# Three hops over a sorted graph beside a dense product: dense units dealt anew over the stages, and hop three's carries and selections a tile ahead

## The chip, the cores and the metric

One core of a Trainium2 chip runs the whole program. The metric is the device time of one execution in microseconds (us). Engines: TensorE (PE; its weight loads are PEld), VectorE (DVE), ScalarE (ACT), GpSimd (POOL), and SyncE (SP), which only issues DMAs. Each engine runs its own list of instructions in order and waits at semaphores.

## The reference

x has 100,000 rows (nodes) of 256 numbers. 25,000 edges, sorted by destination, have a source, a destination and a weight.

```python
feats, cur = [x], x
for _ in range(3):                       # three hops
    msgs = edge_weight[:, None] * cur[src]
    cur = segment_sum(msgs, dst, 100000)
    feats.append(cur)
y = concatenate(feats, axis=1) @ shared_weight + output_bias   # (1024, 256)
out = layernorm(x + y)                   # over each row, without scale or shift
```

Only a fifth of the nodes has an incoming edge, so the product of x with the first 256 rows of the weight (to which the kernel adds the identity, for x + ...) is the bulk, and the three other products are needed for few rows.

## The kernel before

**Dense units.** A unit is 512 rows of x (four to a partition); there are 195 and a tail of 160 rows. Per unit: SP loads x (512 KB, `load_ahead`, six units ahead); PE turns it in two pairs of four transposes (`turn_pair`, L1149) and multiplies it in four parts a pair (`multiply_part`, L1158; a part is two instructions of the trace); ACT copies what is turned (`copy_xT`, L887); DVE adds the bias (`copy_y`, L1441) and takes the statistics (L1447, L1456); ACT takes the root and normalises four rows (`normalise`, L900); SP stores the result (`store_before`).

**Tiles.** Edges lie in 197 tiles of 127, padded to 200; row 0 of a tile holds the carry, the partial sum handed on by the tile before. A tile's sum (`sum_tile`, L1188) multiplies a selection matrix (DVE's `select`, L1597, made from a key row of `keys_bc`) by gathered rows `rows_in`. ACT copies row 0 into the next tile's rows (`carry_into`, L946) and the sum out of PSUM (`copy_sum`, L954). POOL issues the gathers and scatters, which are indirect DMAs (L657, L661, L774).

**Stages**, one behind the other on every engine, with dense units as filler between tiles:

1. Tables, 3 steps of 3 units: sorting tables are built, mostly by DVE.
2. Stage A, hop one, 25 steps of 8 tiles (slots q = 0 to 7) and 3 units. Per tile also the turn of c1 (L1215), its product (`multiply_u`, L1221), DVE's copy to u_out (`copy_u`, L1605), a gather of table rows (`look_up`), `match_tail` (L1610), and per step `rows_found` and `stage_gathers`, which wait for eight semaphores. PE's turn of c1 for tile e-1 waits until DVE has copied u of tile e-3.
3. List, 9 steps of 3 units: the edges that later hops need are listed.
4. Stage B, hop two, 5 steps of 8 tiles and 3 units, and one group of 4 tiles without units.
5. Stage C, hop three: 11 groups of 4 tiles (`group_c`) **without units**. Per tile the sum, the turn of a stored c2 row block and of the sum (L1325), ACT's copy of it (L1052), the product (`multiply_v`, L1332), DVE's copy (`copy_v`, L1890), and POOL's adding scatter to u_rows (`scatter_v`).
6. Stage D, 24 steps of 8 tiles, 23 of them with 3 units; in the 24th the tail unit. Rows with an incoming edge are gathered, multiplied, added to u and written over the stored rows: POOL's `scatter_d` waits for the dense stores below it (`await_stores`). A last loop takes late tiles; it runs once here.

c2_rows is filled with zeros by 50 stores of 512 KB (`zero_c2`, L402), which SP issues in the table steps (24) and the list steps (26). They must be there before stage B scatters. The order of work is the order in which the code writes it for each engine: a slot of PE in stage A is

```python
dense_slot(s, par, turn, q)        # three parts, and turns when a pair begins
sum_tile(e, q % 2, q % G, q)
turn_c1(e - 1, (q - 1) % 2, (q - 1) % Q)
multiply_u(e - 2, q % 2)
```

Of the kernel before, what the change touches and what calls it, by code (L numbers as in the profile page):

```python
def gnn_program(nc, x, src, dst, edge_weight, weight, bias, out):
# [25 lines left out]
    STEPS = UNITS // STEP  # L27
    PAIRS = 2 * UNITS + 1
    assert STEPS * STEP == UNITS and STEPS % 2 == 1
# [17 lines left out]
    A0 = 3  # L47
    A_STEPS = TILES // Q
    A_END = A0 + A_STEPS
    LIST0 = A_END + 3  # L50
    LIST_STEPS = 5
    B0 = LIST0 + LIST_STEPS + 1
    B_STEPS = LIST_STEPS
    D0 = B0 + B_STEPS
    D_STEPS = REAL // Q
    FIRST_GROUPS = 2 * LIST_STEPS
# [3 lines left out]
    assert STEPS - D0 == D_STEPS - 1 and A0 % 2 == 1 and D0 % 2 == 0  # L60
    ZERO_FILLS = TILES // G

# [10 lines left out]
    with ctx:  # L73
# [75 lines left out]
        table_idx = [sb(f"table_idx{k}", [P, Q], i32) for k in range(2)]  # L149
# [8 lines left out]
        record = [sb(f"record{k}", [P, Q, FIELDS], bf16) for k in range(2)]  # L158
# [32 lines left out]
        gather_idx = [sb(f"gather_idx{k}", [P, Q], i32) for k in range(2)]  # L191
# [5 lines left out]

        own_c2 = [u_out[:, k, :] for k in range(G)]
# [23 lines left out]

        blank = sem("blank")
# [9 lines left out]
        keys_loaded = sem("keys_loaded")  # L233
# [6 lines left out]
        tail_keys_stored = sem("tail_keys_stored")  # L240
# [44 lines left out]
        list_stored = sem("list_stored")  # L285
# [76 lines left out]

        def unit_rows(ap, u):
            return ap[bass.ds(u * UROWS, UROWS), :].rearrange("(p r) d -> p (r d)", r=RPP)
# [8 lines left out]
        def _(sp):  # L373
# [15 lines left out]
            def store_before(s, par, k):  # L389

                if not isinstance(s, int) or s >= 1:
                    store_unit(STEP * s - STEP + k, STEP * (1 - par) + k)

            def load_ahead(s, par, k):
                u = STEP * s + k + RING
                if not isinstance(u, int) or u < UNITS:
                    load_unit(u, STEP * par + k)
                elif u == UNITS:
                    load_tail()

            def zero_c2(k):
                sp.dma_start(c2_dram[k * UROWS:(k + 1) * UROWS, :].rearrange("(p r) d -> p (r d)", r=RPP),  # L402
                             zeros[:, :]).then_inc(c2_zeroed, 16)

            def load_keys(a, k):

                until(sp, sel_ready, Q * (a - 1))
                sp.dma_start(keys_bc[k][:, :], keys_out_dram[bass.ds(a * (Q * P), Q * P)].partition_broadcast(P)).then_inc(keys_loaded, 16)
# [38 lines left out]
            load_ahead(0, 0, 0)  # L447
            sp.wait_ge(tail_keys_ready, 1)
            sp.dma_start(tail_keys_dram.rearrange("(h p) c -> p h c", h=2), tail_keys[:, :, :]).then_inc(tail_keys_stored, 16)
            sp.wait_ge(keys_stored, 16)  # L450
            load_keys(0, 0)
            sp.wait_ge(blank, 6)
            for k in range(6):
                zero_c2(k)
            for k in (1, 2):
                load_ahead(0, 0, k)
            zeroed = 6
            for s in (1, 2):
                for k in range(STEP):
                    store_before(s, s % 2, k)  # L460
                    load_ahead(s, s % 2, k)
                    for j in range(3):
                        zero_c2(zeroed + j)
                    zeroed += 3


            def step_a(a, s, par, last=False):
                store_before(s, par, 0)
# [12 lines left out]
                load_ahead(s, par, 2)  # L481

            step_a(0, A0, 1)
            with sp.Fori(A0 // 2 + 1, (A_END - 2) // 2) as h:
                for par in range(2):
                    step_a(2 * h + par - A0, 2 * h + par, par)
            step_a(A_STEPS - 2, A_END - 2, 0)
            step_a(A_STEPS - 1, A_END - 1, 1, last=True)


            def dense_step(s):
                for k in range(STEP):
                    store_before(s, s % 2, k)
                    load_ahead(s, s % 2, k)

            s = A_END
            store_before(s, s % 2, 0)
            store_c1(A_STEPS - 1, 1)
            load_ahead(s, s % 2, 0)
            store_u(A_STEPS - 1, 1)  # L500
            for k in (1, 2):
                store_before(s, s % 2, k)
                load_ahead(s, s % 2, k)
            for s in range(A_END + 1, B0):
                if s == LIST0 - 1:
                    sp.wait_ge(listed_copied, A_STEPS)
                    sp.dma_start(list_dram.rearrange("(p t) f -> p (t f)", p=P),
                                 listed[:, :, :].rearrange("p t f -> p (t f)")).then_inc(list_stored, 16)
                for k in range(STEP):
                    store_before(s, s % 2, k)  # L510
                    load_ahead(s, s % 2, k)
                    for j in range(2):
                        if zeroed < ZERO_FILLS:
                            zero_c2(zeroed)
                            zeroed += 1
            assert zeroed == ZERO_FILLS

# [14 lines left out]
            for b in range(B_STEPS):  # L532
                s, t = B0 + b, Q * b
                store_before(s, s % 2, 0)
# [6 lines left out]
                load_ahead(s, s % 2, 0)  # L541
                store_before(s, s % 2, 1)
                load_ahead(s, s % 2, 1)
                store_c2(t, 0, TILES + t + G)
                store_before(s, s % 2, 2)
                load_ahead(s, s % 2, 2)
# [7 lines left out]

            C_TILE = TILES + G * n_groups
            for half in range(2):
# [4 lines left out]
            def group_c(g):  # L561
                for k in range(G):
# [3 lines left out]
                    if k == G - 2:  # L566
                        load_keys2(G * g + G, G, 0, C_TILE + G * g + G)

            load_keys2(0, G, 0, C_TILE)
            group_c(0)  # L570
            with sp.Fori(1, n_groups) as g:
                group_c(g)
# [10 lines left out]
            def step_d(d, s, par):  # L583
                store_before(s, par, 0)
                load_ahead(s, par, 0)
                store_before(s, par, 1)
                if not isinstance(d, int) or d > 0:
                    load_u(2 * d + 3, (2 * par + 3) % 4)
                load_ahead(s, par, 1)
                store_before(s, par, 2)  # L590
                load_ahead(s, par, 2)
                load_u(2 * d + 4, 2 * par)
# [3 lines left out]
            for d in range(2):  # L596
                step_d(d, D0 + d, d)
            with sp.Fori(D0 // 2 + 1, STEPS // 2 - 1) as h:
                for par in range(2):
                    step_d(2 * h + par - D0, 2 * h + par, par)  # L600
            for d in range(D_STEPS - 4, D_STEPS - 1):
                step_d(d, D0 + d, d % 2)
            for k in range(STEP):
                store_before(STEPS, 1, k)
# [4 lines left out]
            load_u(2 * D_STEPS + 1, (2 * D_STEPS + 1) % 4, 1)  # L609
# [1442 lines left out]
```

## Time and profile before

| | |
|---|---|
| median of 3 runs | 1757.12 us (1756.4 to 1757.37) |
| the profiled execution | 1757.15 us, span 1755.4 us |
| PE busy | 1578.4 us, 90% of the span |
| DVE, ACT, POOL busy | 67%, 65%, 61% |
| DMA | 450.85 MB, mean 257 GB/s |
| chain that ended last | PE 77%, DVE 7%, issue 6%, DMA 4% |

Busy time is what an engine spent in instructions that the profile counts. The time stands beside the span: 1.75 us of it lie outside. A row of a timeline has the start in us, the duration, engine, line, operation, output and inputs, a count of merged instructions, and in brackets the idle time before it and what ended that. The chain's shares are of the whole span; what a change is worth is read stage by stage.

### The profile page before, as it was taken

The numbers are of one execution on the slowest core, as the hardware profiler recorded it, in microseconds if no ns is written. First come the engines' busy times: TensorE is split into PE (matmuls) and PEld (weight loads), VectorE is DVE, ScalarE is ACT, GpSimd is POOL, SyncE is SP. The second block draws the span as 40 slices with busy tenths as digits, with TensorE's granted clock in tenths as the row PEclk, the third lists the DMA queues.
The fourth block names the chain that finished last, engine by engine and source line by source line (L and its number), as shares of the span: only waits on it lengthen the run. The fifth ranks groups of instructions, "written<-read, shape, count | busy, mean of one in ns | idle before, by whom it ended". The sixth has DMA issues, their size and how long they took to land.

```text
span 1755.4 us, 37470 instructions
## 1 busy us (share of the span) xinstructions
PE 1578.4 (90%) x8468; PEld 1337.8 (76%) x8468; DVE 1180.8 (67%) x4883; ACT 1147.7 (65%) x3038; POOL 1065.6 (61%) x1043
## 2 busy tenths in 40 slices
PE   6899999999999999998788477777999999999993
PEld 5688888888888888886677265556888888888872
DVE  6767777777777777788766312224777777777773
ACT  3677778777778777665467323324777777777773
POOL 2266656666656666114567756655777777777765
PEclk9899999999999999999899799998999999999997
DMA  8988888888888888798589655546888887888752
GB/s 291 402 300 274 285 284 269 283 277 270 286 285 269 282 279 272 234 389 340 170 297 344 205 112 108 113 98 216 276 275 272 278 275 273 276 277 275 266 198 96
DMA packets 214099, 450.85 MB, mean 257 GB/s; under 512 B 30044, under 2 KB 125593, under 8 KB 214022
## 3 DMA queue, kind: packets, MB, share of 16 engines
q1 hardware_dynamic: 164130, 343.20, 55.9%
q0 software_dynamic: 49456, 106.58, 21.3%
q8 instruction: 29, 0.48, 0.1%
q14 instruction: 48, 0.39, 0.1%
q10 hardware_dynamic: 436, 0.20, 0.0%
HBM read 232.78 MB, written 225.74 MB: 261 GB/s over the span
## 4 chain that ended last, share of the span: by engine, by line
PE 77%; DVE 7%; issue 6%; DMA 4%; POOL 2%; ACT 2%; DVEq 1%; SPq 1%; ACTq 0%; POOLq 0%
PE ps_y L1158 32%; PE ps_u L1221 9%; PE ps_xT L1149 8%; PE ps_sum L1188 7%; PE ps_sum L1366 5%; PE ps_u L1366 5%; PE ps_y L1332 4%; PE ps_u L1215 3%; DVE y_ring L1441 1%; PE ps_u L1360 1%; DVE stats L1447 1%; DMA entries<-listed_edges,list_idx 1%; PE ps_sum L1360 1%; PE ps_xT L1325 1%; DMA c_rows<-sums,scatter_idx 1%
## 5 line engine op out<-in xcount | busy, mean ns | idle before, releaser
L1158 PE MATMUL ps_y<-w_sb,xT 128*128 128x256 f32 x3128 | 810.9, 386 | 19.7 <-DVE y_ring L1441 18.3
L1158 PEld LDWEIGHTS ps_y<-w_sb,xT 128*128 128x128 f32 x3128 | 564.6, 193 | 80.5 <-issue 17.3
L900 ACT ACTIVATE o_ring<-y_ring,shift,rstd 128x256 f32<-128x256 f32 (+1 forms) x782 | 421.8, 590 | 7.3 <-DMA u_rows<-u_out,scatter_idx 7.3
L887 ACT COPY xT<-ps_xT 128x512 f32<-128x512 f32 x391 | 226.5, 579 | 259.5 <-PE ps_xT L1149 259.2
L1441 DVE TENSOR_TENSOR y_ring<-ps_y,bias 128x512 f32<-128x512 f32 x391 | 269.9, 690 | 166.4 <-PE ps_y L1158 159.4
L657 POOL DMA_INDIRECT tails_found<-tail_keys,table_idx x200 | 200.2, 1001 | 234.1 <-PE ps_sum L1188 119.6
L1447 DVE BATCH_NORM_STATS2 stats<-y_ring 128x6 f32<-128x256 f32 (+1 forms) x782 | 290.8, 414 | 3.4
L1149 PE MATMUL ps_xT<-ident,x_ring 128*128 128x128 f32 x1564 | 238.9, 276 | 24.4 <-ACT xT L887 15.5
L1188 PE MATMUL ps_sum<-rows_in,sel 128*128 128x256 f32 x576 | 181.9, 398 | 83.6 <-ACT rows_in L946 43.8
L657 POOL DMA_INDIRECT rows_in<-in_x,gather_idx x200 | 203.5, 1018 | 83.2 <-issue 78.5
L657 POOL DMA_INDIRECT rows_in<-in_x,tailx_idx x197 | 200.0, 1015 | 76.7 <-issue 44.1
L661 POOL DMA_INDIRECT out_rows<-u_out,tailo_idx x197 | 198.4, 1007 | 79.3 <-issue 39.5
L1149 PEld LDWEIGHTS ps_xT<-ident,x_ring 128*128 128x128 f32 x1564 | 193.7, 142 | 68.0 <-ACT xT L887 18.9
L1221 PE MATMUL ps_u<-w_sb,cT 128*128 128x256 f32 x800 | 205.9, 380 | 0.0
L1188 PEld LDWEIGHTS ps_sum<-rows_in,sel 128*128 128x128 f32 x576 | 103.7, 192 | 111.9 <-issue 89.2
L1221 PEld LDWEIGHTS ps_u<-w_sb,cT 128*128 128x128 f32 x800 | 136.7, 191 | 10.2
L1605 DVE TENSOR_TENSOR u_out<-ps_u,bias 128x256 f32<-128x256 f32 x200 | 84.3, 422 | 82.3 <-PE ps_u L1221 81.0
L954 ACT COPY sums<-ps_sum 128x256 f32<-128x256 f32 x288 | 103.5, 359 | 54.2 <-PE ps_sum L1188 45.0
L946 ACT COPY rows_in<-ps_sum 1x256 f32<-1x256 f32 x285 | 100.3, 352 | 51.2 <-PE ps_sum L1188 44.0
L657 POOL DMA_INDIRECT rows_in<-c_rows,gather_idx x92 | 95.0, 1033 | 40.0 <-issue 26.2
L1077 ACT ACTIVATE u_out<-sums,cshift,crstd 128x256 f32<-128x256 f32 x197 | 116.1, 592 | 0.0
L1597 DVE TENSOR_SCALAR sel<-keys_bc,key_in,w 128x128 f32<-128x128 f32 x288 | 101.4, 356 | 16.2 <-issue 7.5
(227 smaller groups left out, 2074.0 us busy)
## 6 DMA issues: line engine op xcount, KB each, us to landing
x_ring<-in_x SPq DMA_DIRECT2D x195, 512.0 KB, 5.9
out_rows<-o_ring SPq DMA_DIRECT2D x195, 512.0 KB, 3.3
c_rows<-zeros SPq DMA_DIRECT2D x50, 512.0 KB, 9.3
c_rows<-sums SPq DMA_DIRECT2D x50, 512.0 KB
u_rows<-u_out SPq DMA_DIRECT2D x50, 512.0 KB, 4.0
keys_bc<-keys_out SPq DMA_DIRECT2D x30, 512.0 KB, 6.8
keys_bc<-u_rows SPq DMA_DIRECT2D x25, 512.0 KB, 5.6
tails_found<-u_rows SPq DMA_DIRECT2D x12, 512.0 KB
```

Of the source, the lines that this page charges most:

```text
L657: pool.indirect_dma_start(dest, None, table, bass.IndirectOffsetOnAxis(ap=index, axis=0), bounds_check=bound, oob_is_err=False).then_inc(s ...
L661: pool.indirect_dma_start(table, bass.IndirectOffsetOnAxis(ap=index, axis=0), source, None, bounds_check=bound, oob_is_err=False).then_inc ...
L887: act.copy(view[0], view[1]).then_inc(xT_copied, 1)
L900: last = act.activation(o_ring[slot][0:rows, r * D:(r + 1) * D], y_ring[k][0:rows, r * D:(r + 1) * D], ACT.Identity, bias=shift[k][0:rows, ...
L1077: act.activation(co[q], cy[q], ACT.Identity, bias=cshift[half][:, k:k + 1], scale=crstd[half][:, k:k + 1]).then_inc(cnormed, 1)
L1149: last = pe.transpose(ps_xT[:, q * P:q * P + rows], x_ring[slot][0:rows, at:at + P], ident[0:rows, 0:rows])
L1158: last = pe.matmul(ps_y[bank][0:rows, r * D:(r + 1) * D], xT[bank][:, q * P:q * P + rows], w_sb[:, c, :], start=c == 0, stop=c == KC - 1)
L1188: pe.matmul(ps_sum[bank][:, 0:D], sel[k][:, :], rows_in[row][:, :], start=True, stop=True).then_inc(summed, 1)
L1221: last = pe.matmul(ps_u[bank][:, D:2 * D], cT[bank][:, c * P:(c + 1) * P], w_sb[:, KC + c, :], start=c == 0, stop=c == KC - 1)
L1366: last = pe.matmul(ps_tail[q % G][:, D:2 * D], cT[q % 2][:, c * P:(c + 1) * P], w_sb[:, c, :], start=c == 0, stop=c == KC - 1)
L1441: dve.tensor_tensor(y_ring[k][0:rows, half * 2 * D:(half + 1) * 2 * D], ps_y[half][0:rows, :], bias2[0:rows, :], ALU.add).then_inc(y_copie ...
L1447: last = dve.bn_stats(stats[k][0:rows, r, :], y_ring[k][0:rows, r * D:(r + 1) * D])
```

## The change

- **Units anew.** Stage A has two units a step instead of three; a bridge of two units stands between B and C; ten of C's eleven groups have two units; all 24 steps of D have three, and the tail unit goes into the step behind. 9 + 50 + 27 + 15 + 2 + 20 + 72 = 195. Steps are now described by (first unit, units, turns of the loop, units of the step before); `unit_at` gives slots. Loops of A hold three steps instead of two.
- **Zero fills.** All 50 are issued in stage A, two a step.
- **Keys of A** come in halves of 256 KB into three buffers instead of 512 KB into two; `record`, `table_idx` and `gather_idx` have three buffers.
- **Stage C.** Its turns and products move to other PSUM banks (ps_u, ps_list) and to the buffer of tails_found, so that ps_xT, ps_y and xT stay with the dense units. ACT's carry and DVE's selection of tile n+1 stand in tile n. Its ten filled groups are written out, the last is a loop.
- **End.** POOL's scatters of the last full step stand ahead of the wait for all stores.

The constants, the steps, and SP's part of stage A:

```diff
-    A0 = 3
+    TABLE_STEPS = 3
+    A_UNIT = STEP * TABLE_STEPS
     A_STEPS = TILES // Q
...
+    C_UNIT = BRIDGE_UNIT + PAIR
+    D_UNIT = C_UNIT + PAIR * FIRST_GROUPS
...
+        def unit_at(off, turns):
+            return off + RING * turns, off % RING, turns + off // RING, off % STEP
...
+        def a_step(i, turns=0):
+            return A_UNIT + PAIR * i, PAIR, turns, STEP if isinstance(turns, int) and i == 0 else PAIR
...
+            def load_keys(a, half, place):
+                until(sp, sel_ready, Q * a + G * half - 2 * G + 1)
...
+                store_behind(dense, 0)
                 if not isinstance(a, int) or a > 0:
                     store_c1(a - 1, 1)
-                if not last:
-                    load_keys(a + 1, par)
-                load_ahead(s, par, 0)
+                if more:
+                    load_keys(a + 1, 0, (place + 1) % 3)
                 if not isinstance(a, int) or a > 0:
                     store_u(a - 1, 1)
-                store_before(s, par, 1)
-                load_ahead(s, par, 1)
+                load_ahead(dense, 0)
+                store_behind(dense, 1)
+                if more:
+                    load_keys(a + 1, 1, (place + 1) % 3)
+                zero_c2(2 * a)
                 store_c1(a, 0)
-                store_before(s, par, 2)
+                load_ahead(dense, 1)
+                zero_c2(2 * a + 1)
                 store_u(a, 0)
-                load_ahead(s, par, 2)
```

POOL, the last scatters:

```diff
             gather_d(LATE0 + G, G, D_STEPS, D_STEPS % 2)
+            await_stores(UNITS - RING, 0)
+            for k in range(Q):
+                scatter_d(LATE0 - Q + k, k, D_STEPS - 1, (D_STEPS - 1) % 2)
             for k in range(RING):
                 pool.wait_ge(stored[k], 16 * (UNITS // RING + (k <= UNITS % RING)))
                 limit(N)
-            for k in range(Q):
-                scatter_d(LATE0 - Q + k, k, D_STEPS - 1, (D_STEPS - 1) % 2)
```

ACT, the bridge and stage C:

```diff
+            dense_step(bridge_step)
...
+            carry_c(0, 0, True)
+            for n in range(G * FIRST_GROUPS):
+                g, k = n // G, n % G
+                dense_slot(c_step(g), 2 * k)
+                copy_sum_c(n, k)
+                if n + 1 < G * FIRST_GROUPS:
+                    carry_c((n + 1) // G, (n + 1) % G)
+                dense_slot(c_step(g), 2 * k + 1)
+                copy_t(n, k)
```

PE, a dense slot, and stage C:

```diff
-                for m in range(3 * q, 3 * q + 3):
+                for m in range(units * q, units * q + units):
...
+                    if dense is not None:
+                        dense_slot(dense, 2 * k)
                     sum_tile(C_TILE + n, k % 2, k, k)
                     if not isinstance(n, int) or n > 0:
                         multiply_v(n - 1, (k - 1) % 2)
+                    if dense is not None:
+                        dense_slot(dense, 2 * k + 1)
                     pe.wait_ge(own_loaded[k], 16 * g + 16)
```

DVE, stage C:

```diff
+            select_c(0, 0)
+            for n in range(G * FIRST_GROUPS):
+                g, k = n // G, n % G
+                products_c(g, k)
+                if n + 1 < G * FIRST_GROUPS:
+                    select_c((n + 1) // G, (n + 1) % G)
+                for q in (2 * k, 2 * k + 1):
+                    dense_slot(c_step(g), q)
```

**PE in stage A**, slots 4 and 5 of the first step (ps_sum is the tile sum, ps_u the turn and product of c1, ps_xT and ps_y the dense turn and parts). Before:

```order
L1149 MATMUL ps_xT<-ident,x_ring4 128x128 x4
L1158 MATMUL ps_y0<-w_sb,xT0 128x256 x3
L1188 MATMUL ps_sum0<-rows_in4,sel0 128x256
L1215 MATMUL ps_u1<-ident,sums 128x128 x2
L1221 MATMUL ps_u0<-w_sb,cT0 128x256 x2
L1158 MATMUL ps_y0<-w_sb,xT0 128x256
L1149 MATMUL ps_xT<-ident,x_ring5 128x128 x4
L1158 MATMUL ps_y1<-w_sb,xT1 128x256 x2
L1188 MATMUL ps_sum1<-rows_in5,sel1 128x256
```

After:

```order
L1209 MATMUL ps_xT<-ident,x_ring4 128x128 x4
L1218 MATMUL ps_y1<-w_sb,xT1 128x256 x2
L1251 MATMUL ps_sum0<-rows_in4,sel0 128x256
L1278 MATMUL ps_u1<-ident,sums 128x128 x2
L1284 MATMUL ps_u0<-w_sb,cT0 128x256 x2
L1218 MATMUL ps_y1<-w_sb,xT1 128x256 x2
L1251 MATMUL ps_sum1<-rows_in5,sel1 128x256
```

Each slot has two parts instead of three, and a turn in every second slot instead of three of four.

**SP's queue in stage A**, the first step. Before:

```order
L387 DMA out_rows<-o_ring0 128x1024
L408 DMA keys_bc1<-keys_out 128x1024
L379 DMA x_ring3<-in_x 128x1024
L387 DMA out_rows<-o_ring1 128x1024
L379 DMA x_ring4<-in_x 128x1024
L412 DMA c1_rows<-sums 128x4x256
```

After:

```order
L449 DMA out_rows<-o_ring0 128x1024
L480 DMA keys_bc1<-keys_out 128x512
L441 DMA x_ring3<-in_x 128x1024
L449 DMA out_rows<-o_ring1 128x1024
L480 DMA keys_bc0<-keys_out 128x512
L473 DMA c2_rows<-zeros 128x1024
L484 DMA c1_rows<-sums 128x4x256
L441 DMA x_ring4<-in_x 128x1024
L473 DMA c2_rows<-zeros 128x1024
L488 DMA u_rows<-u_out 128x4x256
```

One zero fill now stands ahead of the store of c1, and one ahead of the store of u.

**PE in stage C**, one tile and the next sum. Before (in the first group):

```order
L1188 MATMUL ps_sum1<-rows_in1,sel1 128x256
L1332 MATMUL ps_y0<-w_sb,xT0 128x256 x4
L1325 MATMUL ps_xT<-ident,u_out 128x128 x2
L1325 MATMUL ps_xT<-ident,sums 128x128 x2
L1185 REGISTER_ALU
L1188 MATMUL ps_sum0<-rows_in2,sel2 128x256
```

After:

```order
L1251 MATMUL ps_sum1<-rows_in1,sel1 128x256
L1384 MATMUL ps_u1<-w_sb,tails_found 128x256 x4
L1218 MATMUL ps_y0<-w_sb,xT0 128x256 x2
L1377 MATMUL ps_u0<-ident,u_out 128x128 x2
L1377 MATMUL ps_u0<-ident,sums 128x128 x2
L1209 MATMUL ps_xT<-ident,x_ring2 128x128 x4
L1218 MATMUL ps_y1<-w_sb,xT1 128x256 x2
```

Two parts stand between product and turn, and two more, with a dense turn in every tile, between turn and next sum.

## Rows read from the trace of the kernel before

**Rows 1.** The page's 40 slices of the span, PE's busy tenths
```profile
PE   6899999999999999998788477777999999999993
```

**Rows 2.** Windows, us: length; busy (count) of PE PEld DVE ACT POOL; PE clock, DMA share, GB/s
```profile
30.00:45.00 15.00, 10.20 (x55) 8.64 (x54) 13.95 (x49) 7.12 (x15) 1.99 (x2) 0.94 1.03 416
...
125.00:699.00 574.00, 568.59 (x3188) 486.84 (x3188) 426.32 (x1877) 441.18 (x1335) 352.30 (x349) 1.00 0.85 279
...
900.00:960.00 60.00, 55.80 (x291) 46.86 (x289) 41.92 (x155) 45.61 (x120) 46.24 (x46) 1.00 1.00 364
...
990.00:1000.00 10.00, 0.00 (x0) 0.00 (x0) 0.62 (x4) 0.00 (x0) 7.49 (x8) 0.50 0.51 163
...
1010.00:1180.00 170.00, 122.60 (x595) 99.63 (x595) 37.00 (x167) 51.34 (x127) 106.62 (x81) 0.99 0.53 110
```

**Rows 3.** Line L1188 in 120 to 720, then PE's timeline at a step's boundary
```profile
L1188 PE MATMUL ps_sum<-rows_in,sel x364: 378/379/463, 122.2 to 717.1; 128*128 128x256 f32 x182
...
302.58 0.59 PE L1188 MATMUL ps_sum<-rows_in,sel 128*128 128x256 f32 x2
...
304.15 0.63 PE L1149 MATMUL ps_xT<-ident,x_ring 128*128 128x128 f32 x4
304.62 1.46 PE L1158 MATMUL ps_y<-w_sb,xT 128*128 128x256 f32 x6
305.92 0.59 PE L1188 MATMUL ps_sum<-rows_in,sel 128*128 128x256 f32 x2
307.04 0.44 PE L1215 MATMUL ps_u<-ident,sums 128*128 128x128 f32 x2 [0.53 <-DVE u_out L1605]
```

**Rows 4.** PE's timeline in stage C: start, duration, instruction, [idle before]
```profile
1018.65 0.67 PE L1188 MATMUL ps_sum<-rows_in,sel 128*128 128x256 f32 x2 [0.97 <-DVE sel L1597]
1019.16 1.89 PE L1332 MATMUL ps_y<-w_sb,xT 128*128 128x256 f32 x8
1020.88 0.38 PE L1325 MATMUL ps_xT<-ident,u_out 128*128 128x128 f32 x2
1021.10 0.38 PE L1325 MATMUL ps_xT<-ident,sums 128*128 128x128 f32 x2
...
1178.41 0.69 PE L1188 MATMUL ps_sum<-rows_in,sel 128*128 128x256 f32 x2 [1.11 <-ACT rows_in L946]
```

**Rows 5.** DVE's timeline at the same boundary of stage A
```profile
302.78 0.69 DVE L1441 TENSOR_TENSOR y_ring<-ps_y,bias 128x512 f32<-128x512 f32 x1 [0.75 <-PE ps_y L1158]
...
305.79 0.23 DVE L1435 TENSOR_SCALAR gather_idx<-src_node 128x8 int32 x1 [0.80 <-DMA rows_in<-in_x,gather_idx]
...
306.57 0.42 DVE L1605 TENSOR_TENSOR u_out<-ps_u,bias 128x256 f32<-128x256 f32 x1
```

**Rows 6.** POOL's timeline in stage A
```profile
310.81 1.00 POOL L657 DMA_INDIRECT tails_found<-tail_keys,table_idx  x1 [0.30 <-PE ps_sum L1188]
312.11 0.99 POOL L657 DMA_INDIRECT rows_in<-in_x,gather_idx  x1 [0.30 <-issue]
```

**Rows 7.** Timelines from B to C: PE's first sum, POOL's first gather
```profile
1005.62 1.22 PE L1188 MATMUL ps_sum<-rows_in,sel 128*128 128x256 f32 x2 [16.47 <-DVE sel L1597]
...
1002.10 1.04 POOL L657 DMA_INDIRECT rows_in<-c_rows,gather_idx  x1 [2.47 <-issue]
```

**Rows 8.** Timelines: PE at D's first turn and tail unit; POOL at the end
```profile
1197.45 0.69 PE L1360 MATMUL ps_u<-ident,rows_in 128*128 128x128 f32 x2 [12.25 <-DMA rows_in<-in_x,tailx_idx]
...
1700.34 0.44 PE L1149 MATMUL ps_xT<-ident,x_ring 80*128 80x80 f32 x4
...
1719.85 0.98 POOL L661 DMA_INDIRECT out_rows<-u_out,tailo_idx  x1 [0.30 <-DMA out_rows<-o_ring]
...
1735.27 1.05 POOL L657 DMA_INDIRECT rows_in<-in_x,latex_idx  x1 [0.31 <-ACT u_out L1077]
...
1744.50 0.97 POOL L661 DMA_INDIRECT out_rows<-u_out,lateo_idx  x1 [0.49 <-issue]
```

**Rows 9.** The page's DMA issues: the stores of u_out
```profile
u_rows<-u_out SPq DMA_DIRECT2D x50, 512.0 KB, 4.0
```

More of the change, by code:

```diff
@@ L452, in _ @@
-            sp.wait_ge(blank, 6)
[L453 to L468, printed above, removed]
+            for half in range(2):
+                load_keys(0, half, 0)
@@ L469, in step_a @@
+            for k in (1, 2):
+                load_ahead(table_step(0), k)
+            for s in range(1, TABLE_STEPS):
+                store_and_load(table_step(s))
+            sp.wait_ge(blank, 6)
+            def step_a(a, dense, place):
+                more = not isinstance(a, int) or a < A_STEPS - 1
+                store_behind(dense, 0)
                 if not isinstance(a, int) or a > 0:
                     store_c1(a - 1, 1)
-                if not last:
-                    load_keys(a + 1, par)
@@ L813, in scatter_d, with await_stores, step_d @@
                 scatter(out[:, :], co[q], tailo_idx[par][:, q:q + 1], scattered[q // 2])
-            def await_stores(turn, par):
+            def await_stores(off, turns):
                 for k in range(STEP):
-                    pool.wait_ge(stored[STEP * par + k], 16 * turn)
+                    u, slot, turn, place = unit_at(off + k, turns)
+                    pool.wait_ge(stored[slot], 16 * turn + 16)
                     limit(N)
-            def step_d(d, turn, par, gathers=LATE0):
+            def step_d(d, dense, par, turn, gathers=LATE0):
+                off, units, turns, before = dense
                 for q in range(Q):
@@ L977, in _, with step_a @@
             for q in range(4, Q):
-                dense_slot(2, 0, 1, q)
-            def step_a(a, s, par, turn, last=False):
+                dense_slot(table_step(2), q)
+            def step_a(a, dense, place):
                 for q in range(Q):
@@ L1078, in c_normalise, with step_d @@
                                scale=crstd[half][:, k:k + 1]).then_inc(cnormed, 1)
-            def step_d(d, dense=None):
+            def step_d(d, slot=None):
                 for q in range(Q):
@@ L1085, in step_d @@
                         copy_ta(n - 1, (q - 1) % Q)
-                    if dense is not None:
-                        dense(q)
+                    if slot is not None:
+                        slot(q)
                     if q % G == 2 and (not isinstance(g, int) or 0 < g <= -(-REAL // G)):
@@ L1341, in group_c @@
                         multiply_v(n - 1, (k - 1) % 2)
+                    if dense is not None:
+                        dense_slot(dense, 2 * k + 1)
                     pe.wait_ge(own_loaded[k], 16 * g + 16)
@@ L1344, in group_c @@
                     until(pe, t_copied, n)
[L1345 to L1348 removed]
+                    turn_rows(ps_t, (own_c2[k], sums[:, k, :]), t_psum)
+            for g in range(FIRST_GROUPS):
+                group_c(g, c_step(g))
+            with pe.Fori(FIRST_GROUPS, n_groups) as g:
                 group_c(g)
```

624 lines of the change are left out of this document (306 added, 318 removed).

## The prediction

> **What bounds the kernel now.** I read the page's slices first [rows 1]. The digit of PE is 9 nearly everywhere; it drops at the very start, in four or five slices in the middle, and at the end. So TensorE is the bound in most of the kernel, and time can be won only where it stands still. The table by stages says where [rows 2]. In stage A (hop one, 125 to 699) PE is busy 568.6 of 574 us at a granted clock of 1.00. In stage C (hop three, 1010 to 1180) it is busy 122.6 of 170, while DVE (37) and ACT (51) are mostly idle: nothing is full there, it is a chain of waits. At the end of stage B, 990 to 1000, PE does nothing.
>
> Two periods are needed. 182 tiles of stage A begin from 122.2 to 717.1 [rows 3], so a tile takes 594.9/181 = 3.29 us and a step of eight 26.29. In stage C tile sums start at 1018.65 and, 40 tiles on, at 1178.41 [rows 4]: 3.99 us a tile. Between those starts PE's own work is the sum (0.51 to the next start), the product (1.72) and two times two turns (0.22 each), 2.67 us; it waits 1.32 us of each tile, and the row at 1178.41 names ACT's carry, the copy of row 0 for the next sum.
>
> A dense unit costs PE four groups of four turns and sixteen parts. Four turns take 2 x 0.22 = 0.44 [rows 4]; six parts' instructions take 1.30 from 304.62 to 305.92 [rows 3], so a part (two instructions) is 0.433. Two pairs of (0.44 + 4 x 0.433): 4.33 us a unit.
>
> **Part one: stage A, three units to two a step, 25 steps.** PE sheds 4.33 us a step. Not all of it comes back, since PE already waits once a step. Its turn at 307.04 came 0.53 to 0.69 us late, for DVE's copy of u [rows 3]. DVE gets there late because at the end of slot 7 it runs through a copy of y begun at 302.78, statistics, the small copies of rows_found, a pass over eight semaphores ahead of gather_idx at 305.79 (0.80 of idle), and then the copy of u at 306.57 [rows 5]. None of these depends on how many units a step has: slot 7 ends with a pair in both versions. PE needs 3.77 us from the sum at 302.58 to the end of the sum at 305.92 + 0.43, and of this the change takes one part, 0.43 (three parts to two). So the wait grows by 0.43 and the step ends at 26.29 - 4.33 + 0.43 = 22.39. **A: -25 x 3.90 = -97.5 us.** Bounds: nothing lost, -108.3; everything lost (another resource holds the step at 26.29), 0. I take the value near the first end, since PE is the bound in 99% of this stretch.
>
> Can the others keep up at 22.39? POOL issues 16 indirect transfers a step, 1.30 us from start to start [rows 6]: 20.8, so yes, by 1.6 us. ACT's share was 441 of 574 us and it loses a unit's copies too; DVE's was 426 [rows 2]. The DMA volume doesn't fall. A step now moves eleven 512 KB transfers (three loads, three stores, keys, two of c1, two of u), eight gathers of 128 KB and eight of 64 KB: 7.34 MB, and 7.34/26.29 = 279 GB/s, the figure of the row. The change takes out two transfers and puts in two zero fills of the same size, which sat before in the table and list stages. So the step must run at 7.34/22.39 = 328 GB/s. Two rows are near: 900 to 960 ran at 364 GB/s, with POOL's gathers and scatters still issued every 1.3 us, and 30 to 45 at 416 [rows 2]. I price this at nothing; its cover is that x is loaded six units ahead and the stores of c1 and u have four to five slots to land.
>
> The zero fills leave the table and list stages. I take 0 there: the table stage ends with DVE's chain (13.95 of 15 us busy in 30 to 45 [rows 2]), and the list stage is alike. A gain up to 3 us is possible.
>
> **Part two: stage C gets two units a group of four tiles, in ten of eleven groups.** PE's work per tile becomes 2.67 + 2.17 = 4.84 us, more than the 3.99 of today. The 1.32 us wait should vanish: in the new order ACT does carry n+1 directly after copying sum n, DVE selects for n+1 in tile n, and 3 us of other PE work stands between. ACT's work would be 1.2 us a tile as now (51.3 of 170 for 42.6 tiles) and half a unit, at most 3.4 (in A three units and eight tiles together take it 441/574 x 26.29 = 20.2): 4.6, below 4.84. POOL has two instructions. The new waits are: PE's dense turn queues ahead of the sum, and ACT's xT copy ahead of the copy of the sum; behind them stand the turn of c rows and all later. I take 4.85. **C: +40 x (4.85 - 3.99) = +34.4.** Bounds: +31 (4.76, if the sum takes its 0.43 of stage A), and +87 if none of the wait is hidden (40 x 2.17). I take the low one, because in stage A the same pieces between sums leave PE busy 99%.
>
> **Part three: a bridge of two units** between B and C, 8.7 us of PE. PE stands idle 16.47 us until the sum at 1005.62, and POOL's first gather of C goes out only at 1002.10 [rows 7]. The bridge begins at 989.2. SP's loads of keys and rows for C stand behind it, and DVE stages the gathers behind it. At the full clock it ends near 999. But the clock granted in 990 to 1000 is 0.50 [rows 2], the lower level of 1.2 GHz, after PE's sparse sums. A part of the bridge runs slowly: I take +1, with 0 to +6 as bounds. The Trainium skill, "TensorE: Matmul & The Clock Gate", section "What's actually happening", says that the throttled state is the default and activity releases it; if no release came in the bridge, its 8.7 would be 17.3, ending at 1006.5, and this term would be near +5 instead of +1. The row's 0.50 agrees with the default; no row here shows the release in that place.
>
> **Part four: the last stage.** Stage D keeps 23 full steps of (1700.34 - 1197.45)/23 = 21.87 us [rows 8] and gets a 24th, and the tail unit moves into the step behind it. Four parts left over from the pair before, which ran before C, now run in D's first step, in the 12.25 us that PE waits there for the first gather [rows 8]: 0. Before, the end hangs on POOL's queue: its wait on the last stores passes at 1719.85, 19.5 after the last dense work began at 1700.34; and from the late gather (1735.27) to the last scatter (1744.50) are 9.2 us. After, the scatters of the last full step stand ahead of the wait on stores, so the end is 21.87 + 19.5 + 9.2 = 50.6 after that same point instead of 44.2: **+6.4**, between 0 and +12.
>
> **Sum.** -97.5 + 34.4 + 1 + 6.4 = -55.7. The profiled execution has a span of 1755.4 and a time of 1757.15 (1.75 outside the span), 0.03 from the median of 1757.12. 1755.4 - 55.7 + 1.75 = **1701.4 us**. As a check: all PE work stays; the idle removed is 40 x 1.3 = 53 in C, 8 at the bridge, 7 at the end, less 11 new in A.
>
> **Rivals.**
> 1. *No growth of the wait in A* (DVE, with a unit less, arrives earlier than its order suggests): 1701.4 - 10.8 = 1690.6. For it: DVE is busy only 74% there. Against: the copy of y at the end of slot 7 starts from PE in both.
> 2. *A becomes partly bound by transfers*: the trace gives 0.85 as DMA share in A [rows 2], and 0.85 x 26.29 = 22.3 us of queue time a step, as long as the new step. For it: that sum. Against: shares of 1.00 and more with 364 and 416 GB/s, so that the share counts packets stretched by each other. At 1 us a step: 1726.4.
> 3. *C isn't filled*: half the 1.32 us wait stays in every tile, since ACT's o_ring normalisations stand before its copies: 5.5 us a tile, +26: 1727.4.
> 4. *Slower than before*: in A the store of u's first half stands in SP's queue behind a zero fill and a load, and DVE may not write u for the next step's first tile until it has landed. It lands in 4.0 us now [rows 9], and has some 12. If it needs more than about 15 us, the step stays above 24.6 us, and from there (42/25 = 1.7 us a step of the 3.9 left) the whole change loses. With the step at 26.29: 1798.9. Against: zero fills in bursts and landings near 10 us would be needed at each step.
> 5. *It doesn't do what it says*: the units in C only push the sums apart with no overlap (+87 instead of +34): 1754.
>
> **Chances.** Forecast 0.46; rival 1, 0.17; 2, 0.17; 3, 0.12; 4, 0.05; 5, 0.03. The range must reach rivals 1 to 3 and the lower ends of the bridge and tail: 1684 to 1734, with rivals 4 and 5 outside. A measurement of this kernel can tell about 0.2%, 3.5 us, from no change. Faster: all but rival 4 and half of 5, 0.93; within 0.2%: 0.02; slower: 0.05.
>
> **What would show it.** In the new profile the tile sums of A should be 2.80 us apart, with PE waiting about 1.1 us a step for DVE's u_out at the first turn of a step, GB/s near 328; those of C 4.85 apart with PE over 95% busy; the first gather of C 15 us or less behind the last sum of B; the last scatter about 51 us behind the start of D's 24th step. Sums in A over 3.0 apart with waits on landings show rival 2 or 4. C over 5.3 apart with waits on ACT shows rival 3.

## The result: 1740.9 us, in the predicted direction, 39 us short of the forecast

The changed kernel takes 1740.87 us (median of 4 runs, 1738.98 to 1743.44), the kernel before 1757.24 (4 runs). The ratio is 0.9907 with a 95% interval of 0.989 to 0.9924: 16 us are gained, where I had forecast 56, and the time lies above my range. The profiled execution has a span of 1737.0.

First the page of the changed kernel: the 40 slices, and the queues that fetch instructions.

```profile
PE   6899898988989899986986999969999999999993
...
q8 instruction: 35, 0.57, 0.1%
q14 instruction: 84, 0.68, 0.1%
```

Against [rows 1], the sevens of hop three (slices 24 to 28) have become nines, but for slice 27, where the last stage begins; but eights have come into hop one (up to slice 16), which was all nines. The second instruction queue has 84 packets (8.1 KB each); the kernel before had 48.

A table of windows follows, between the same landmarks in both kernels: the first and last tile sum of hop one, the first of hop two, the first of hop three, the first turn of the last stage, the turn of the tail unit, the end. Columns as in [rows 2]. After:

```profile
70.54:669.11 598.57, 553.01 (x3003) 464.99 (x3004) 397.65 (x1791) 421.13 (x1332) 392.29 (x391) 0.97 0.88 300
669.11:825.80 156.69, 132.45 (x720) 111.34 (x718) 132.44 (x600) 90.79 (x195) 57.24 (x57) 0.97 0.65 218
825.80:947.16 121.36, 101.94 (x495) 83.14 (x495) 72.03 (x272) 80.83 (x207) 88.29 (x87) 0.94 0.87 306
947.16:1169.33 222.17, 205.34 (x1099) 181.18 (x1099) 98.85 (x416) 116.32 (x272) 116.70 (x92) 0.98 0.73 190
1169.33:1695.39 526.06, 526.06 (x2867) 454.51 (x2867) 404.52 (x1569) 390.63 (x922) 378.57 (x373) 1.00 0.79 266
1695.39:1737.00 41.61, 15.05 (x61) 10.88 (x59) 13.43 (x61) 17.51 (x42) 19.29 (x20) 0.67 0.26 92
```

| stretch | before, us | after, us | difference | forecast |
|---|---|---|---|---|
| start to first tile sum | 73.36 | 70.54 | -2.8 | 0 |
| hop one | 646.88 | 598.57 | -48.3 | -97.5 |
| list stage | 166.00 | 156.69 | -9.3 | 0 |
| hop two and bridge | 119.38 | 121.36 | +2.0 | +1 |
| hop three, to the last stage | 191.83 | 222.17 | +30.3 | +34.4 |
| last stage and end | 557.95 | 567.67 | +9.7 | +6.4 |
| sum | 1755.40 | 1737.00 | -18.4 | -55.7 |

The before column is read from the same windows of its trace. One line is wrong by far: in hop one half of the gain is missing.

### The profile page after: what moved, and what is told of

Same layout as the page of the kernel before. It is cut to its first block, busy times and chain, and to the rows that moved or that the text cites. A ratio compares the mean times of both kernels' runs of the same rounds, so it can differ in the third digit from the quotient of the medians.

```text
span 1737.0 us, 37008 instructions
## 1 busy us (share of the span) xinstructions
PE 1582.6 (91%) x8468; PEld 1346.1 (77%) x8468; DVE 1174.0 (68%) x4883; ACT 1148.5 (66%) x3038; POOL 1064.9 (61%) x1044
## 4 chain that ended last, share of the span: by engine, by line
PE 71%; DVE 10%; issue 8%; DMA 5%; POOL 3%; ACT 1%; DVEq 1%; POOLq 0%; SPq 0%; ACTq 0%
PE ps_y L1218 30%; PE ps_xT L1209 7%; PE ps_u L1284 7%; PE ps_sum L1251 5%; PE ps_sum L1423 5%; PE ps_u L1423 5%; PE ps_u L1278 2%; PE ps_list L1384 2%; PE ps_u L1384 2%; DVE stats L1498 2%; DVE y_ring L1492 2%; POOL rows_in L707 2%; DMA rows_in<-in_x,gather_idx 1%; DMA c_rows<-sums,scatter_idx 1%; PE ps_u L1417 1%
## 5 line engine op out<-in xcount | busy, mean ns | idle before, releaser
L1284 PE MATMUL ps_u<-w_sb,cT 128*128 128x256 f32 x800 | 211.1, 387 | 0.0
L1251 PEld LDWEIGHTS ps_sum<-rows_in,sel 128*128 128x128 f32 x576 | 107.8, 194 | 53.4 <-issue 22.2
L820 POOL DMA_INDIRECT u_rows<-u_out,scatter_idx x44 | 69.0, 1568 | 87.6 <-PE ps_sum L1251 31.9
L1278 PE MATMUL ps_u<-ident,sums 128*128 128x128 f32 x400 | 79.7, 282 | 44.9 <-DVE u_out L1657 43.9
```

Source lines behind the costliest of these rows:

```text
L1251: pe.matmul(ps_sum[bank][:, 0:D], sel[k][:, :], rows_in[row][:, :], start=True, stop=True).then_inc(summed, 1)
L1278: last = pe.transpose(ps_u[bank][:, c * P:(c + 1) * P], sums[:, k, c * P:(c + 1) * P], ident[:, :])
L1284: last = pe.matmul(ps_u[bank][:, D:2 * D], cT[bank][:, c * P:(c + 1) * P], w_sb[:, KC + c, :], start=c == 0, stop=c == KC - 1)
```

## Where hop one lost its gain

VectorE's timeline of the changed kernel shows it, at the end of one step and at the start of the next. Here the releaser named is a landing gather.

```profile
274.45 0.18 DVE L1677 SCALAR_TENSOR_TENSOR active<-place_found,not_padding 128x8 f32 x1
274.67 0.17 DVE L1680 TENSOR_SCALAR inactive<-active 128x8 f32<-128x8 f32 x1
280.76 0.17 DVE L1486 TENSOR_SCALAR gather_idx<-src_node 128x8 int32 x1 [5.92 <-DMA rows_in<-in_x,gather_idx]
```

TensorE pays for it right behind, its timeline and windows over the same place:

```profile
275.32 0.59 PE L1251 MATMUL ps_sum<-rows_in,sel 128*128 128x256 f32 x2
282.00 0.69 PE L1278 MATMUL ps_u<-ident,sums 128*128 128x128 f32 x2 [6.08 <-DVE u_out L1657]
282.48 1.91 PE L1284 MATMUL ps_u<-w_sb,cT 128*128 128x256 f32 x4
...
286.98 1.03 PE L1284 MATMUL ps_u<-w_sb,cT 128*128 128x256 f32 x4
```

```profile
262.00:274.00 12.00, 11.95 (x72) 9.93 (x69) 9.24 (x41) 9.85 (x33) 8.82 (x9) 1.00 0.97 332
274.00:282.00 8.00, 1.92 (x14) 1.42 (x12) 1.95 (x12) 1.85 (x6) 2.09 (x2) 0.84 0.87 317
282.00:292.00 10.00, 10.00 (x43) 8.52 (x44) 4.96 (x24) 5.23 (x17) 5.13 (x6) 0.78 0.28 83
292.00:304.00 12.00, 11.97 (x69) 9.97 (x68) 9.32 (x41) 9.85 (x33) 8.85 (x9) 1.00 0.92 307
```

Behind the 6 us of standing still TensorE's granted clock is 0.78 over ten microseconds: four matmuls take 1.91 us at the lower level (1.2 GHz), 1.03 at the full one. So one such place costs twice. It comes back with a fixed period. These are starts of gather_idx on VectorE, one a step:

```profile
252.85 0.17 DVE L1486 TENSOR_SCALAR gather_idx<-src_node 128x8 int32 x1 [0.42 <-issue]
280.76 0.17 DVE L1486 TENSOR_SCALAR gather_idx<-src_node 128x8 int32 x1 [5.92 <-DMA rows_in<-in_x,gather_idx]
305.35 0.17 DVE L1486 TENSOR_SCALAR gather_idx<-src_node 128x8 int32 x1 [0.42 <-issue]
327.82 0.17 DVE L1486 TENSOR_SCALAR gather_idx<-src_node 128x8 int32 x1 [0.42 <-issue]
355.58 0.17 DVE L1486 TENSOR_SCALAR gather_idx<-src_node 128x8 int32 x1 [5.77 <-DMA rows_in<-in_x,gather_idx]
```

The undisturbed step is 22.47 us (305.35 to 327.82), close to my 22.39. Three steps are 74.82 here (280.76 to 355.58) instead of 67.4: 7.4 to 7.5 us are lost every third step. And three steps are one turn of the new loop. The trace of the line of that loop (L409) has VectorE's branches:

```profile
L409 DVEq COMPARE_BRANCH  x7: 50/67/72, 199.9 to 649.9; - x7
```

Six of the seven are taken, and behind each the next record of VectorE comes 5.20 to 5.41 us later. In the kernel before (nine taken) it is 0.28 to 0.33 us. Between two branches lie 387 records of VectorE; before, with two steps a turn, 301. No view names this cause. The releaser in the row is merely the last semaphore of the eight that VectorE looks at there (one of the six rows says "issue").

**Theory 1**: VectorE's loop body has become too long to be kept, and at each branch back its top must be fetched again. The Trainium skill, "Runtime: NRT & Kernel Launch", section "Instruction fetch mechanics", describes this: a taken branch to a page outside the window forces a fetch before execution goes on. It gives an engine like VectorE 512 instructions, in two blocks of 256. By that, a body of 387 can stay or not, as it happens to lie over the blocks; the 5.2 us behind each branch say that here it doesn't. Rivals: **theory 2**, transfers are late at 330 GB/s, and the releaser is right; **theory 3**, one step in three is longer by its own work.

## The experiments

**1. VectorE's hop one written out** (e1), and **2. the other four engines' instead** (e2):

```diff
         def each_a_step(eng, run, flat=False):
+            if flat:
+                for a in range(A_STEPS):
+                    run(a, a_step(a), a % 3)
+                return
...
-            each_a_step(dve, step_a)
+            each_a_step(dve, step_a, flat=True)
```

> The changed kernel with VectorE's loop of hop one written out as 25 steps; instructions, waits and their order are the same, only the loop's branch is gone. Theory 1 (the branch back to the top of a long loop body costs VectorE 5.4 us, and TensorE then runs 2.1 us more at a lower clock): the six idles of 5.7 to 5.9 us before gather_idx vanish, every step of hop one takes 22.47 us, and the time falls by 6 x 7.5 = 45 us, from 1740.9 to about 1696. Theory 2 (the idle is a wait for landing gathers, as the releaser in the row says, because transfers are late at 330 GB/s): the idles stay, time within 3 us of 1740.9. Theory 3 (one step in three is longer by its own work): the same as theory 2.

> The mirror of the first: SyncE, GpSimd, ScalarE and TensorE have hop one written out, VectorE keeps its loop of three steps. Theory 1 in the form that only VectorE's branch matters: six idles of 5.4 us or more on VectorE stay, time within 3 us of 1741. If the branches of the other engines had a part in it (theory 1b): the time falls by some of the 45 us, below 1730. Theory 2: 1741.

Measured: e1 1682.26 us (4 runs, ratio to before 0.9584, 0.9567 to 0.9601), e2 1740.39 (one run) with the six idles of 5.69 to 5.99 us still there. Windows of e1:

```profile
125.00:590.00 465.00, 462.77 (x2594) 390.31 (x2593) 342.64 (x1576) 360.51 (x1148) 342.49 (x340) 1.00 0.98 335
```

```profile
219.96 0.17 DVE L1490 TENSOR_SCALAR gather_idx<-src_node 128x8 int32<-128x8 int32 x1 [0.20 <-issue]
...
241.81 0.37 DVE L1490 TENSOR_SCALAR gather_idx<-src_node 128x8 int32<-128x8 int32 x1 [0.20 <-issue]
```

Theories 2 and 3 fall: the same instructions and the same transfers, at 335 GB/s, leave TensorE busy 462.8 of 465 us. The gain is 58.6 us, not 45: the step is 21.85 us (219.96 to 241.81), 0.62 less than the undisturbed looped one. So a looped step has a cost of its own: the idle ahead of gather_idx is 0.42 us in the loop and 0.20 written out, and TensorE's 0.5 us wait for u_out at the top of a step is gone. 6 x 7.5 + 21 x 0.62 = 58.

**3. The length of the body by itself.** Only the kernel before is padded here, in VectorE's loop of two steps: with waits already satisfied (e3), then with 86 and with 64 one-column memsets (e5, e6).

```diff
+                    if not isinstance(a, int):
+                        for z in range(86 * (Q * par + q) // (2 * Q), 86 * (Q * par + q + 1) // (2 * Q)):
+                            dve.memset(scratch[:, z:z + 1], 0.0)
                     dense_copy(s, q)
```

> The kernel before, with 86 waits that are already satisfied spread over VectorE's loop body of two steps (5 or 6 a slot of about 3.3 us; each takes about 0.1 us of VectorE, which idles a quarter of the time): 301 records a turn become 387, as many as the changed kernel's body of three steps. Nothing else changes. Theory 1: an idle of about 5.4 us at the top of the body at each of 9 branches back, 9 x 7 = 60 us longer, about 1815. Theories 2 and 3: no such idles; 1757, or a few us more for the waits themselves (up to 9 us a turn of VectorE's time, mostly in its idle time).

> The last padding run was no fair test: its 86 waits came out as 40 more records a turn (301 to 341), not 86. Here the kernel before gets 86 one-column memsets of a scratch tile in VectorE's loop body of two steps, 5 or 6 a slot, which cannot be merged: 387 records, as in the changed kernel's body. Theory 1 (length of the body): about 5.4 us of idle at each of 9 branches, and 2 us of TensorE at a lower clock behind each: 60 to 70 us longer than 1756.5, about 1820, plus what the memsets themselves cost. Theory 1c (not the length, but something else in the new order, as the branch's place): no idle at the branches, below 1775.

> The same with 64 memsets: 365 records a turn, between 341 (no idle at the branch) and 387. It only narrows the bound. If 365 is too long too: idles of about 5.4 us at 9 branches and a time near 1815; if not: below 1770. Theory 1c expects the latter in both.

e3 took 1753.78 us, but most of its waits came out two to a record, so the body had 341. e6 (365 records): 1755.33, no idle at the branches. e5 (387): 1789.77, 33 us more than before. Its VectorE at one branch, and its instruction queue beside that of e6:

```profile
260.10 0.17 DVE L1436 TENSOR_SCALAR gather_idx<-src_node 128x8 int32 x1 [3.48 <-issue]
```

```profile
q14 instruction: 95, 0.77, 0.1%
```

```profile
q14 instruction: 48, 0.39, 0.1%
```

Between 365 and 387 records a turn the price appears, and with it the extra packets of the instruction queue (95; 48 in e6, as in the kernel before). That 22 more memsets a turn should cost 34 us by themselves is ruled out by e6: its 64 cost nothing to be seen. So the length decides, in a kernel with none of the change in it. That what is paid for is a fetch is read from the packets and not shown in any other way. The bound of 365 to 387 holds for this place in the program: whether it also matters where the body starts was not tested. The price was mis-sized: the gap behind each of the nine taken branches is 2.80 to 3.08 us, not 5.4.

**4. Is the price per branch?** VectorE's loop turns 4 times instead of 7, the other nine steps are written out (e14). And **is it the load of the queues?** The changed kernel, loop and all, with the zero fills back in the table and list stages (e15).

```diff
-            with eng.Fori(0, A_TURNS) as h:
+            with eng.Fori(0, turns) as h:
...
-            for a in range(A_LAST, A_STEPS):
+            for a in range(A_FIRST + A_TURN * turns, A_STEPS):
```

> VectorE's loop turns 4 times instead of 7, the other 9 steps are written out, again: 3 branches back and 12 looped steps. With 7.5 us a branch back and 0.62 a looped step: 1682.3 + 22.5 + 7.4 = 1712. If the price were not per branch: near 1741 or near 1682.

> The changed kernel with its loop and the zero fills back in the table and list stages, again: hop one moves about 270 GB/s instead of 299 on average over its loop. Theory L (the fetch waits behind data): the gap behind the branch falls from 5.3 us towards 3. Theory S (it is of what has to be fetched): 5.2 to 5.4, and about 1748.

e14 took 1711.8 us (one run) against 1712 expected: the two prices, 7.5 us a branch back and 0.62 us a looped step, add up. The packets of the second instruction queue follow the branches too: 65 in e1, 75 in e14 with three taken, 84 with six. e15 took 1741.41. Its hop one, and one of its branches:

```profile
125.00:651.00 526.00, 485.57 (x2643) 406.72 (x2642) 353.19 (x1601) 367.00 (x1164) 347.38 (x347) 0.97 0.78 259
```

```profile
281.48 0.17 DVE L1499 TENSOR_SCALAR gather_idx<-src_node 128x8 int32 x1 [4.96 <-DMA rows_in<-in_x,gather_idx]
```

With 259 GB/s instead of 299 the gap behind the branch falls from 5.20-5.41 us (5.16-5.46 in e2, 4.99-5.39 in e14) to 4.38-4.95. By this one run, load is a part of it, but not all: e5, at 263 GB/s, pays 2.8 to 3.1 with the same 387 records. What makes up the rest stays open.

**5. The zero fills, without the stall** (e4): e1 with the 50 fills back where they were, 24 in the table stage and 26 in the list stage.

```diff
-                zero_c2(2 * a)
                 store_c1(a, 0)
                 load_ahead(dense, 1)
-                zero_c2(2 * a + 1)
```

> The first of these kernels (VectorE's hop one written out) with the 50 zero fills back where they were before the change: 24 in the table stage, 26 in the list stage, none in hop one. Theory 2 (transfers hold hop one): its steps go below 22.4 us, and hop one gains more than the fills cost elsewhere. Theory 1: steps of hop one stay within 0.2 us of 22.47. In both the list stage, from the last tile sum of hop one to the first of hop two, goes back from 156.7 us to about 166, if the fills were what made it longer before (I had put their move at 0 to -3 us), and the whole is some 9 us slower than the first kernel: about 1705.

1688.78 us (one run), 6.5 more than e1, where I expected some 9. The list stage, last sum of hop one to first of hop two, is 163.6 us (612.43 to 776.06), in e1 156.2 (611.06 to 767.23). Hop one doesn't get faster without the fills: TensorE is busy 462.8 of 465 us in both.

```profile
125.00:590.00 465.00, 462.83 (x2595) 390.35 (x2595) 342.71 (x1575) 359.89 (x1146) 343.23 (x340) 1.00 0.88 287
```

**6. The kernel before with VectorE's hop one written out** (e7), to see what the change is worth without any loop.

```diff
-            with dve.Fori(A0 // 2 + 2, (A_END - 2) // 2) as h:
-                for par in range(2):
-                    step_a(2 * h + par - A0, 2 * h + par, par)
+            for a in range(3, A_STEPS - 2):
+                step_a(a, A0 + a, (A0 + a) % 2)
```

> The kernel before with VectorE's hop one written out. The first experiment gained 58.6 us where the six idles with what follows them are 45; its steps took 21.85 us instead of 22.47, with TensorE waiting nowhere. If the loop's register arithmetic (VectorE's 0.3 to 0.8 us of idle before gather_idx at each step, then TensorE's 0.53 to 0.69 us) is what the other 13 us are: the steps of before fall from 26.29-26.35 to 25.8, 20 steps in the loop, about 10 us, and the time from 1756.5 to about 1746. Against a written-out loop in both, the change is then worth 1746 - 1682 = 64 us. If the register arithmetic is no cost: 1756.5.

1747.88 us (4 runs, ratio 0.9951, 0.9935 to 0.9968): 9.1 us for 20 looped steps, where I expected 10. Its steps are 25.85 us, those of e1 21.85: a unit less is 4.00 us. Written out on both sides, the change is worth 0.9584/0.9951, or 65 us.

**7. Hop three, "a tile ahead" undone** in e1: carry and selection in the tile's own turn (e8), then the carry alone (e16).

```diff
-            carry_c(0, 0, True)
             for n in range(G * FIRST_GROUPS):
                 g, k = n // G, n % G
+                carry_c(g, k, n == 0)
                 dense_slot(c_step(g), 2 * k)
                 copy_sum_c(n, k)
-                if n + 1 < G * FIRST_GROUPS:
-                    carry_c((n + 1) // G, (n + 1) % G)
...
-            select_c(0, 0)
             for n in range(G * FIRST_GROUPS):
                 g, k = n // G, n % G
+                select_c(g, k)
                 products_c(g, k)
-                if n + 1 < G * FIRST_GROUPS:
-                    select_c((n + 1) // G, (n + 1) % G)
```

> The first experiment's kernel (1682.3) with one part of the change undone in hop three: ScalarE makes the carry of a tile, and VectorE its selection, in that tile's own turn, ahead of its dense slots, instead of a tile ahead; the dense units stay. Theory A (the early carry is what lets a tile take only TensorE's own 4.77 us): ScalarE's carry for the next tile then comes behind a whole dense part, the copy of t and stands late, so TensorE waits at each sum, 0.5 to 1.3 us a tile, 20 to 50 us longer. Theory B (three microseconds of dense work between the sums hide it in any order): within 3 us of 1682.

> VectorE's hop one written out, and in hop three ScalarE's carry in the tile's own turn while VectorE's selection stays a tile ahead, again. Theory Q (the late selection blocked SyncE's queue in e8): no waits for own rows, within 10 us of 1682.3. Theory R (the late carry delays all): above 1700, with waits for ScalarE's rows_in.

e8 took 1750.66 us, 68 more than e1 and more than I expected; e16 1682.76, no more than e1 (one run each). From the first sum of hop three to the last are 268.5 us in e8 and 203.4 in e1. TensorE stands idle for 49.1 of them against 4.9, and is busy 20.8 us longer with the same matmuls, at a granted clock of 0.95 instead of 0.99. Its waits in e8 between 947 and 1160, and SyncE's queue there:

```profile
PE ps_u L1379 <- DMA u_out<-c_list_rows: 25.4, 8, 4.1
PE ps_sum L1253 <- DVE sel L1651: 9.8, 16, 0.6
PE ps_sum L1253 <- ACT rows_in L1010: 3.6, 3, 1.3
```

```profile
977.46 0.43 SPq L621 DMA_DIRECT2D u_out<-c_list_rows  x1
989.26 0.33 SPq L577 DMA_DIRECT2D keys_bc<-keys_out  x1
989.63 0.43 SPq L453 DMA_DIRECT2D out_rows<-o_ring  x1
990.10 0.43 SPq L621 DMA_DIRECT2D u_out<-c_list_rows  x1
```

The next group's keys overwrite those of this group, so SyncE issues their load only behind the last selection of the group. One tile later, its queue stands for 11.8 us (977.46 to 989.26), with the own rows of the next tiles behind it, and TensorE waits for those once a group. With the late carry alone (e16) nothing is lost. So it is the selection a tile ahead that makes hop three work, by letting SyncE's queue go on; the early carry is worth nothing that one run shows. The late selection without the late carry was not run.

**8. All five engines written out** (e13).

> Hop one written out on all five engines, again (the last call's chip ran the kernel before at 1957 us). On a chip where the kernel before takes 1757: TensorE was busy 462.8 of 465 us in hop one with VectorE alone written out, so 1682 within 3 us; if the other engines' loops still cost something, up to 5 us less.

1685.88 us (4 runs, ratio 0.9591, 0.9575 to 0.9607), not to be told from e1: the other engines' loops cost nothing that these runs show. e1 and e13 beat both kernels of the case; e1 needs the smaller edit.

**9. Another chip.** The four kernels of experiments 8, 4 and 7 (e13 to e16) also ran, as e9 to e12, on a chip on which the kernel before takes 1957.47 us (13 runs).

> The changed kernel with hop one written out on all five engines. In the first experiment (VectorE alone written out, 1682.3) TensorE was busy 462.8 of 465 us of hop one, so nothing is left to gain there: 1682, within 3 us. If register arithmetic of TensorE or the others still held hop one: up to 5 us less.

There the written-out kernel took 1954.74 us (10 runs, ratio 0.999, 0.9958 to 1.0023), e10 1992.89, e11 1996.52 and e12 1972.55 (one run each). Windows of e9, then of e1, over the same stretch of hop one:

```profile
200.00:400.00 200.00, 174.85 (x961) 142.98 (x960) 124.51 (x573) 132.15 (x424) 125.19 (x125) 1.00 0.86 291
```

```profile
200.00:400.00 200.00, 199.37 (x1119) 168.37 (x1118) 147.40 (x678) 153.79 (x491) 147.45 (x147) 1.00 0.98 338
```

The clock is full, but TensorE is busy 87% instead of nearly 100, with 291 GB/s instead of 338. VectorE itself is no slower: its mean instruction takes 0.217 us in both. The 73 us that this kernel gains in e13 come to 3 on that chip, within its noise. This fits my second rival (hop one bound by transfers), though I have not shown that transfers are what is slow there. The gap behind VectorE's taken branches is there too, and more scattered: 3.9 to 4.6 us in e10, 2.8 to 4.7 in e11, which has no zero fills in hop one.

## The prediction, step by step

- **What bounds the kernel**: right. The time was won where TensorE had stood still, and hop one was full but for one short wait in every second step.
- **Hop one**: "So the wait grows by 0.43 and the step ends at 26.29 - 4.33 + 0.43 = 22.39". The undisturbed step is 22.47, but by luck: errors nearly cancel. A unit was worth 4.00 us, not 4.33 (25.85 - 21.85 in e7 and e1; I haven't traced the difference). And "PE already waits once a step" was misread. The 0.53 us at 307.04 [rows 3] stand right behind a branch. At the top of the step before, the turn comes right behind the sum:

```profile
279.84 0.60 PE L1188 MATMUL ps_sum<-rows_in,sel 128*128 128x256 f32 x2
280.45 0.44 PE L1215 MATMUL ps_u<-ident,sums 128*128 128x128 f32 x2
```

  So the kernel before had the wait in every second step of its loop (0.52 to 0.60 us), with the period of the loop; the changed one has 0.47 to 0.57 us in every undisturbed looped step, some 0.25 more on average and not 0.43. The "0.53 to 0.69" were two measures of one wait.
- **The step that failed** is the next one: "**A: -25 x 3.90 = -97.5 us**" took one step's length times 25. Measured is -48.3. I counted what each engine does in a step, but not what the loop around the steps does. The diff said it: a loop of three steps for one of two. The 0.80 us of idle ahead of gather_idx [rows 5], which I read as a pass over eight semaphores, was in part the price of the loop: 0.80 behind a branch, 0.33 in the step between, 0.20 written out. Six branches at 7.5 us are 45 of the 49 us missing.
- **"Can the others keep up"** was answered right: e1 runs at 335 GB/s with TensorE full. Rival 2 was wrong on these chips. A first reading of "DMA rows_in" as the releaser would have spoken for it.
- **Zero fills**: "I take 0 there" was too careful. Start and list stage together gained 12.1 us; the list stage's part was 7.5 in e4 against e1. In that stage the kernel before moves 401 GB/s and TensorE is busy 36.48 of 40 us in this window:

```profile
760.00:800.00 40.00, 36.48 (x196) 30.40 (x195) 35.70 (x152) 26.00 (x56) 12.05 (x13) 1.00 1.02 401
```

- **Hop three**: "The 1.32 us wait should vanish" is right. Sums are 4.76 us apart, TensorE is full, and I took 4.85:

```profile
957.38 0.59 PE L1251 MATMUL ps_sum<-rows_in,sel 128*128 128x256 f32 x2
...
962.14 0.59 PE L1251 MATMUL ps_sum<-rows_in,sel 128*128 128x256 f32 x2
...
966.90 0.59 PE L1251 MATMUL ps_sum<-rows_in,sel 128*128 128x256 f32 x2
```

- **Bridge**: +3.7 us between the last sum of hop two and the first of hop three (21.33 for 17.66), within my 0 to +6 but above +1, and hop two gave 1.7 back. The first gather comes 17.8 us behind the last sum, not 15. The bridge starts at the lower clock, as I feared: the granted clock is 0.51 from 927 to 931.5, and eight matmuls (four parts) take 3.62 us there, 1.89 later. That is about 2 of the 2.8 us; the rest was not traced.

```profile
927.70 3.62 PE L1218 MATMUL ps_y<-w_sb,xT 128*128 128x256 f32 x8
...
943.63 1.04 POOL L707 DMA_INDIRECT rows_in<-c_rows,gather_idx  x1 [4.42 <-issue]
947.16 1.22 PE L1251 MATMUL ps_sum<-rows_in,sel 128*128 128x256 f32 x2 [7.34 <-DVE sel L1649]
```

- **The end**: +9.7 for +6.4; the last scatter comes 52.7 us behind the start of the 24th step, 51 forecast.
- **Rivals**: none named the branch. The time fell between rival 3 (1727.4) and rival 5 (1754), and by no mechanism on the list. Without the six stalls the kernel would be, by my estimate, at 1740.9 - 45 = 1696, inside the range. That too would be partly luck, since it holds the 12.1 us of the start and list stages that I put at 0. With all of the loop's price gone (e1, 1682.3) it lies just below the range.

## What to carry to other kernels

When a change makes a loop body longer, count each engine's records per turn, not only the work per step: one engine's body can stop fitting at once (here between 365 and 387 records on VectorE), and then every turn pays, and TensorE's clock on top. The sign in a profile is an idle at the same first instruction of the loop, with the period of the loop and not of the data, and a releaser that is not to be believed. More packets of the instruction queue go with it, but are no proof alone: writing out the other four engines' loops adds packets too (65 in e1, 82 in e13), without costing time. Writing out the loop on that one engine is the cheapest test, and here the cure.

A part such as "make it a tile ahead" should be costed by which queue its semaphore lets go on, not only by the engine that computes it.

## What the hardware showed that I had not expected

- VectorE branches back in 0.3 us with 301, 341 (0.28 to 0.33 each) or 365 records in the body, and in 2.8 to 5.4 us with 387. ScalarE with 282 and TensorE with 489 records in its sequencer showed no such gap.
- Straight-line code of 25 steps on VectorE showed no such gap, and 65 packets of the second instruction queue where the loop of three steps took 84.
- The six microseconds without work cost TensorE about 2 more afterwards: the granted clock is 0.78 over the 10 us behind, and the step behind a stall is 24.59 us instead of 22.47 (280.76 to 305.35).
- Between chips, the same kernel before took 1757 and 1957 us.
